# Neighbour counts turned by DMA transposes, and broadcast rows made by TensorE transposes, in a two-layer graph network kernel

## What is computed

```
x1  = layernorm(x + gcn(x, edges))           # normalised by degree, W is 768 x 768
h1  = relu(layernorm(gat(x1, W1, 4 heads x 256))) + x1 @ Wr1 + br1
h2  = layernorm(gat(h1, W2, 1 head x 768)) + h1 @ Wr2 + br2
out = layernorm(x1 + h2)

gat: xl = x @ W;  a_src, a_dst = sums of xl with two vectors, for each head
     e  = leaky_relu(a_src[src] + a_dst[dst], 0.2)
     softmax of e over the edges into each dst, then the weighted sum of xl[src], plus a bias
```

## Time and profile before

| | |
|---|---|
| three runs | 844.8, 844.95, 847.12 us; median 844.95 |
| the profiled execution | 844.18 us, its span 842.3 us, so 1.9 us lie around the span |
| mean granted TensorE clock | 0.994 |
| PE busy | 808.9 us, 96% of the span |
| DVE busy | 672.1 us, 80% |
| ACT, POOL busy | 268.8 and 60.1 us |
| DMA | 73.55 MB, 87 GB/s over the span |

### The profile page before, as it was taken

How to read it: one execution, slowest core, us unless ns; L and a number is a source line. 1 busy time by engine, 2 the same in 40 slices (tenths; PEclk the granted TensorE clock), 3 DMA queues, 4 the chain that set the end, 5 groups by cost and what they waited for, 6 DMA issues and landing times.

```text
span 842.3 us, 13750 instructions
## 1 busy us (share of the span) xinstructions
PE 808.9 (96%) x5022; PEld 533.0 (63%) x5022; DVE 672.1 (80%) x1181; ACT 268.8 (32%) x510; POOL 60.1 (7%) x81
## 2 busy tenths in 40 slices
PE   5899998999999999999999998999999999999995
PEld 4577774665554444447888887886666666555553
DVE  7999995777676659999988879969872287996686
ACT  2454456010011201015555455643301107760000
POOL 3000002011103000000000000011110000001111
PEclk9999999999999999999999999999999999999998
DMA  8000004041131353235212104113223342112232
GB/s 306 7 2 2 2 3 170 25 162 57 45 156 70 100 178 124 82 120 201 61 59 86 53 1 138 57 63 126 88 63 94 124 137 76 65 57 75 75 113 71
DMA packets 24588, 73.55 MB, mean 87 GB/s; under 512 B 2756, under 2 KB 3756, under 8 KB 24398
## 3 DMA queue, kind: packets, MB, share of 16 engines
q1 hardware_dynamic: 23262, 67.61, 23.3%
q0 software_dynamic: 1264, 5.11, 1.8%
HBM read 52.40 MB, written 20.31 MB: 86 GB/s over the span
## 4 chain that ended last, share of the span: by engine, by line
PE 89%; DVE 5%; issue 3%; DVEq 2%; ACT 1%; DMA 0%; POOL 0%; SPq 0%; POOLq 0%
PE psum L957 19%; PE psum L984 19%; PE psum L750 18%; PE psum L1065 12%; PE psum L872 8%; PE psum L762 6%; PE psum L814 3%; PE psum L972 1%; PE psum L998 1%; DVEq L1359 1%; PE psum L909 1%; PE psum L937 1%; ACT arena L1072 1%; PE psum L807 1%; PE psum L723 1%
## 5 line engine op out<-in xcount | busy, mean ns | idle before, releaser
L984 PE MATMUL psum<-arena 128*128 128x257 f32 x800 | 175.4, 381 | 2.6 <-DVE arena L1601 1.6
L1072 ACT ACTIVATE arena<-psum 128x160 f16<-128x160 f32 (+6 forms) x188 | 93.4, 528 | 258.9 <-PE psum L750 74.8
L984 PEld LDWEIGHTS psum<-arena 128*128 128x128 f32 x800 | 151.2, 190 | 26.2 <-ACT arena L1072 2.7
L750 PE MATMUL psum<-arena 128*128 128x512 f16 x720 | 159.3, 379 | 2.3 <-DVE arena L1429 1.9
L957 PE MATMUL psum<-arena 128*128 128x512 f16 x960 | 158.5, 326 | 0.2 <-ACT arena L1072 0.2
L957 PEld LDWEIGHTS psum<-arena 128*128 128x128 f16 x960 | 93.5, 97 | 62.3 <-ACT arena L1072 0.5
L750 PEld LDWEIGHTS psum<-arena 128*128 128x128 f16 x720 | 69.3, 98 | 86.4 <-issue 7.0
L1065 PE MATMUL psum<-arena 128*128 128x512 f16 (+2 forms) x600 | 98.4, 326 | 0.0
L1065 PEld LDWEIGHTS psum<-arena 128*128 128x128 f16 x600 | 58.3, 97 | 39.8
L1457 DVE CUSTOM_DVE_ANT_0 arena<-arena 128x1280 bf16<-128x1280 bf16 x50 | 71.0, 1488 | 14.1 <-DMA arena<-as_scratch 8.2
L1175 ACT ACTIVATE arena<-arena 128x640 f32<-128x640 f32 x80 | 64.5, 836 | 49.4 <-DVE arena L1586 49.2
(11 more groups left out here) (173 smaller groups left out, 714.9 us busy)
## 6 DMA issues: line engine op xcount, KB each, us to landing
arena<-in_L_gnn_W_dram SPq DMA_DIRECT2D x22, 384.0 KB, 3.2
r_scratch<-arena SPq DMA_DIRECT2D x10, 512.0 KB, 2.6
arena<-uv_scratch SPq DMA_DIRECT2D x16, 320.0 KB, 4.4
arena<-r_scratch SPq DMA_DIRECT2D x10, 512.0 KB, 3.7
x_scratch<-arena SPq DMA_DIRECT2D x10, 384.0 KB, 4.5
arena<-x_scratch SPq DMA_DIRECT2D x10, 384.0 KB, 3.5
r_scratch<-arena SPq DMA_DIRECT2D x10, 384.0 KB, 2.6
arena<-r_scratch SPq DMA_DIRECT2D x10, 384.0 KB, 3.7
```

The costliest lines, as they stand in the source:

```text
L750: ins = pe.matmul(o[:, a:b], part[:, k, ds(t * P, P)], w[:, k, a:b], start=(not begun and k == 0 and n == 0 and m == 0), stop=(k == kn - 1 ...
L984: last = pe.matmul(p_att[:, ATT_BANKS[ch][j], 0:HID + 1], pf[n % PSLOTS][:, j * P:(j + 1) * P], xl[ch % H][:, k, 0:HID + 1], start=(k == 0 ...
L1072: act.activation(out_, in_, ACT.Copy, scale=scale).then_inc(signal, 1)
```

## The change

- `c_hi` is stored whole to HBM (`c_d`) after the third load of W1. When the first aggregation is over, ten DMA transposes (`dma_start_transpose`, 128 rows x 1280 columns each) bring it back turned, as `c_turned`, f16 at 70 KB, in the place of `c_lo`.
- The ten `neg` steps leave `X1_ORDER`. `tr 2` now stands after tile 0, `tr 3` after tile 1.
- `mask` reads `c_turned` in SBUF instead of PSUM, and writes `neg` over it. Its wait is for all ten transposes. Four masks stand after the eviction of tile 2, three after tile 3, three after tile 4 (`MASKS_AT`).
- `xl_evict(0)` stands directly behind tile 0's sums, and waits for the store of `c_hi`.
- On SP the store of the masks moves behind the first two loads of Wr1.
- `rows_of` uses `pe.transpose` instead of `pe.matmul`, with the same operands.

```
-        X1_ORDER += [s for k in range(KD) for s in [("part", 0, k)] + ([("neg", k - 3)] if k >= 3 else [])] + [("xl", 0)]
-        X1_ORDER += [s for k in range(KD) for s in [("part", 1, k)] + [[("neg", 3)], [("tr", 2)], ...][k]] + [("xl", 1)]
+        X1_ORDER = [("tr", 0), ("tr", 1)] + [("part", 0, k) for k in range(KD)] + [("tr", 2), ("xl", 0)]
+        X1_ORDER += [("part", 1, k) for k in range(KD)] + [("tr", 3), ("xl", 1)]
...
             sp.wait_ge(S["h_done"], T)
-            weights(1)
+            weights(1, range(3))
+            sp.wait_ge(S["blk_free"], NB)
+            sp.dma_start(c_d, c_hi.rearrange("p t n -> p (t n)")).then_inc(S["c_out"], 16)
+            weights(1, range(3, KD))
...
+            sp.wait_ge(S["c_out"], 16)
+            sp.wait_ge(S["gcn_done"], T)
+            for k in range(T):
+                sp.dma_start_transpose(c_turned[:, :, k * P:(k + 1) * P], c_d[:, k * NP:(k + 1) * NP]).then_inc(S["c_turn"], 16)
+            sp.wait_ge(S["x1_out"], 16 * T)
+            sp.wait_ge(S["x1_tr"], T)
+            weights(2, range(2))
             sp.wait_ge(S["neg_ok"], T)
             sp.dma_start(neg_d, neg.rearrange("p t n -> p (t n)")).then_inc(S["neg_out"], 16)
-            sp.wait_ge(S["x1_out"], 16 * T)
-            sp.wait_ge(S["x1_tr"], T)
-            weights(2)
+            weights(2, range(2, KD))
...
-                elif what == "neg":
-                    slot_read(t, used[t % 2])
-                    for k in range(T):
-                        last = pe.transpose(p_neg[t % 2][:, k * P:(k + 1) * P], c_hi[:, k, t * P:(t + 1) * P], ident_h)
-                    last.then_inc(S["neg_tr"], 1)
-                    used[t % 2] = (what, t)
...
-                    last = pe.matmul(o[:, i * P:(i + 1) * P], column[:, t:t + 1].to_broadcast([P, P]), ident, start=True, stop=True)
+                    last = pe.transpose(o[:, i * P:(i + 1) * P], column[:, t:t + 1].to_broadcast([P, P]), ident)
...
-                dve.wait_ge(S["neg_tr"], t + 1)
-                dve.tensor_scalar(neg[:, t, :], p_neg[t % 2], 0.0, NEG_BIG, ALU.is_equal, ALU.mult).then_inc(S["neg_ok"], 1)
+                dve.wait_ge(S["c_turn"], 16 * T)
+                dve.tensor_scalar(neg[:, t, :], c_turned[:, t, :], 0.0, NEG_BIG, ALU.is_equal, ALU.mult).then_inc(S["neg_ok"], 1)
...
                 elif what == "xl":
-                    if t == 1:
-                        dve.wait_ge(S["par_b1"], 16)
-                        xl_evict(0)
                     dve.wait_ge(S["xl_done"], t + 1)
                     project(t, H, HID, p_x[t % 2], a_junk)
-                    if t:
-                        xl_evict(t)
+                    if t == 0:
+                        dve.wait_ge(S["par_b1"], 16)
+                        dve.wait_ge(S["c_out"], 16)
+                    xl_evict(t)
+                    for m in MASKS_AT.get(t, ()):
+                        mask(m)
```

More of the change, by code:

```diff
@@ L89 @@
 AHEAD_R = 2
+MASKS_AT = {2: range(0, 4), 3: range(4, 7), 4: range(7, T)}
 WR1_AT = {5: (0,), 6: (1, 2), 7: (3,), 8: (4, 5)}
@@ L261, in gnn_program @@
         x1_sb = x_sb
+        c_turned = at(70 * KB, [T, NP], f16)
         neg = at(70 * KB, [T, NP], bf16)
@@ L336, in gnn_program @@
         p_deg, p_flag = bank(7, 2 * T), psum[0:1, 512 * 7 + 32:512 * 7 + 33]
-        p_neg = [psum[:, 512 * i:512 * i + NP // 2].bitcast(f16) for i in (6, 0)]
         p_out = [psum[:, 1024 * i:1024 * i + D] for i in range(2)]
@@ L351, in gnn_program @@
         r2_d = nc.dram_tensor("r2_scratch", [T, P, D], f32).ap()
+        c_d = nc.dram_tensor("c_scratch", [P, T * NP], f16).ap()
         neg_d = nc.dram_tensor("neg_scratch", [P, T * NP], bf16).ap()
@@ L365, in gnn_program @@
             w_in0 w_in1 w_in2 w_in3 w_in4 w_in5 w_hi w_lo clo_ok deg_done dinv_ok over_ok flag_done flag_ok
-            neg_tr neg_ok gcn_done gcn_read gcn_var gcn_rstd x1_ok x1_out
+            c_out c_turn neg_ok gcn_done gcn_read gcn_var gcn_rstd x1_ok x1_out
             x1_tr x1t_hi_ok x1t_lo_ok as_ok as_tr as_rows as_dram asr0 asr1 max_ok
@@ L405, in step_count @@
             return steps_done, enter_loop, leave_loop
-        X1_ORDER = [("tr", 0), ("tr", 1)]
-        X1_ORDER += [s for k in range(KD) for s in [("part", 0, k)] + ([("neg", k - 3)] if k >= 3 else [])] + [("xl", 0)]
-        X1_ORDER += [s for k in range(KD) for s in [("part", 1, k)] + [[("neg", 3)], [("tr", 2)], [("neg", 4), ("tr", 3)], [("neg", 5), ("neg", 6)], [("neg", 7)], [("neg", 8), ("neg", 9)]][k]] + [("xl", 1)]
+        X1_ORDER = [("tr", 0), ("tr", 1)] + [("part", 0, k) for k in range(KD)] + [("tr", 2), ("xl", 0)]
+        X1_ORDER += [("part", 1, k) for k in range(KD)] + [("tr", 3), ("xl", 1)]
         X1_ORDER += [s for i in range(2, T) for s in [("tr", t) for t in (2 * i, 2 * i + 1) if t < T] + [("xl", i)]]
@@ L643, in _ @@
             param("par_b1", b1, 2)
-            pool.wait_ge(S["neg_tr"], T)
+            pool.wait_ge(S["gcn_done"], T)
+            pool.wait_ge(S["c_out"], 16)
             pool.wait_ge(S["w_lo"], W_FIRST[2])
@@ L890, in slot_read @@
             def slot_read(t, last):
-                if last and last[0] == "neg":
-                    pe.wait_ge(S["neg_ok"], last[1] + 1)
-                elif last:
+                if last:
                     pe.wait_ge(S["x1t_lo_ok"], last[1] + 3)
@@ L1485, in _ @@
                     x1t_low(t)
-                elif what == "neg":
-                    mask(t)
                 elif what == "xl":
-                    if t == 1:
-                        dve.wait_ge(S["par_b1"], 16)
-                        xl_evict(0)
                     dve.wait_ge(S["xl_done"], t + 1)
                     project(t, H, HID, p_x[t % 2], a_junk)
-                    if t:
-                        xl_evict(t)
+                    if t == 0:
[4 more added lines that the diff above has]
+                        mask(m)
                     weights(2, WR1_AT.get(t, ()))
```

## The result

The changed kernel takes **836.93 us**, the median of 4 runs (836.0 to 838.46), against 846.0 us of the kernel before on the same chip (844.8 to 847.12). The ratio is 0.9895, with a 95% interval of 0.9871 to 0.9919: faster by 9.1 us, 1.1%. Forecast were 834.0 us and a gain of 10.7 us in the trace; the profiled spans differ by 8.1 us.

The account below looks back on a forecast made before the run. TensorE, holding 89% of the chain, was taken as the bound. 842.3 - 7.3 - 3.4 = 831.6 us of span, 833.5 for the profiled execution, 834.3 on the median's scale; said 834.0, range 832.0 to 852.0.

Parts of the forecast that it names:

- Part 1: TensorE's path through x1 @ W1: without the count transposes tile 4 starts at 245.6 instead of 252.92, a gain of 7.3 us.
- Part 2: VectorE in x1 @ W1: masks of 0.82 us each fit beside TensorE's tiles and cost nothing; b1 has 9 us to spare.
- Part 3: Storing the counts to HBM, 3200 KB in 9.0 us, costs nothing, with 20 us of cover before SP's next load.
- Part 4: The ten DMA transposes before the masks: taken to land within 28 us of issue, so no stall of TensorE.
- the rivals: For the transposes: landing 28.4 to 39 us after issue, late yet a gain (13%); from 39 us, slower than before (22%).
- mostly bytes: Argument on the DMA transposes: a packet's time is mostly bytes, so a 256 B run costs far less than 0.135 us.
- the forecast deadline: The last DMA transpose may land at 240.0, 28.4 us after issue; each later microsecond costs TensorE one.
- the 22% for a loss: Rival at the first mask: transposes land 39 us or more after issue, making the kernel slower, 859.6 to 914 us; chance 22%.
- Part 5: Broadcast rows in layer two: ten transposes take 1.09 us instead of 2.23, saving 3.4 us over three calls.
- all that hangs on the end of tile 9 moves with it: After x1 @ W1: sums, their row over HBM, Wr1 products and attention all start earlier by the full 7.3 us.
- the second attention near 723.3: Sign in layer two that the forecast holds: the second attention starts 10.7 us earlier, near 723.3.
- a gain given back before 733: Sign of being wrong: the gain in x1 @ W1 is lost again before 733 on the trace's clock.

Follow-up runs that it names:

- b_same: The kernel before with nothing changed, run again for a second trace: 846.48 us, ratio 1.001 to before.
- rows_only: The kernel before with only the broadcast rows made by transposes instead of products: 842.18 us, ratio 0.9961 to before.
- late_turn: The changed kernel with five of the ten DMA transposes sent twice, the masks waiting for the second set: 840.57 us, ratio 0.9937 to before.
- store_first: tr3_early with the 40 KB store of the finished row issued ahead of two weight loads on SP: 836.28 us, ratio 0.9879 to before.
- tr3_early: The changed kernel with tile 3's transposes put in the middle of tile 1's matmuls: 833.63 us, ratio 0.9857 to before; repeated, 835.14 us, 0.9867.

## Why the prediction was nearly right, point by point

**Part 1, TensorE's path: right.** Tile 4 was forecast for 245.6 and came at 246.13. The 0.5 us are 0.13 us of the wait of `tr 5` (1.33, not 1.2), 0.2 of its own length (0.85, not 0.65), 0.13 in tile 0 and the rest in hundredths.

**Part 2, VectorE: right in its result, with a term too large.** The masks cost 0.42 us each and not 0.82; the nearer row was the one within SBUF, 648 elements in 324 ns, and even the 0.64 us by that row are half as much again as was measured. Since they were hidden, nothing came of it but 1.6 us of slack. b1 needed 5.8 us instead of 3.7 and had 9 to spare.

**Part 3, the store of the counts: nothing, as said.** It took 14.7 us where 9.0 were taken from the store of the masks, and so landed at 151.6, 14 us ahead of SP's next load. The cover did it, not the estimate.

**Part 4, the transposes: right, and the rivals fell.** Landing 22.6 us after the issue, within the 28.4. The argument that a small run costs less than the mean packet held (0.028 against 0.135 us); that its cost is "mostly bytes" did not: at 145 GB/s with full engines it costs 2.6 times what its bytes cost at the 383 GB/s of the earlier trace rows. The margin was 5.8 us against the forecast deadline, so the 22% for a loss were not foolish. The Trainium skill's *DMA: Bandwidth & Descriptors* ("Latency and other measured facts") with its 261 GB/s, which the page gives for a non-contiguous middle dimension, gave 12.6 us by the estimate in part 4; measured were 22.6, and the 12.8 us are what a plain load of the same bytes took here. The Trainium skill's *VectorE: DVE Perf Modes* ("The three transpose paths") with 1309 ns a block gave 131 us by the other estimate there; measured were 0.226 us a block, a hundred blocks in 22.6 us. For this stream of ten pieces neither figure holds, and the measured one decides.

**Part 5, the broadcast rows: right to the hundredth.** 1.09 us a call, 3.43 us in three calls, in every pair of traces with and without them. The Trainium skill's *TensorE: Matmul & The Clock Gate* (terms table) would have made it 0.56 us by its factor of four, an estimate; the trace shows 2.05 times (2.23 against 1.09 us), not four times.

**The step that failed: "all that hangs on the end of tile 9 moves with it".** It moved, but not by as much. In the profiles of before and after, from tile 4 to the attention:

| event | before | after | earlier by |
|---|---|---|---|
| tile 4 | 252.92 | 246.13 | 6.8 |
| first maximum (`as_scratch` is back) | 312.90 | 307.36 | 5.5 |
| store of the finished row issued | 371.92 | 366.11 | 5.8 |
| its load issued | 375.46 | 370.81 | 4.7 |
| attention | 383.76 | 379.08 | 4.7 |

1.3 us went with the first trip of the row over HBM and 1.2 us with the store of the second; 0.3 us came back between, where the kernel before had let TensorE finish its matmuls ahead of the row. I had read the chain of before, seen only TensorE in it, and took what ran beside it for covered. It had no cover, as VectorE's timeline of the kernel before shows:

```profile
380.40 2.48 DVE L1586 SCALAR_TENSOR_TENSOR arena<-arena 128x640 f32<-128x640 f32 x3 [0.30 <-DMA arena<-uv_scratch]
```

VectorE did wait for the row, 0.30 us, and with 2.48 us for these and 0.75 for the next step its factors were ready at 383.6, a tenth or two before TensorE was free. The sum should have held a term of 0 to 2 us for that. Some of the 2.1 us is that the first trace of before caught short transfers; the measured times, from several runs each, show a gain of 9.1 us, 1.6 us short of the forecast.

The means of the traces have the same size. From tile 4 to the attention the three with counts turned by TensorE (before, `b_same`, `rows_only`) take 131.85 us and the nine with DMA transposes 133.4. Of these 1.55 us, 1.0 lies between the issue of the two weight loads and the landing of the second store (4.66 against 5.68, two groups that don't touch), and 0.6 in the first trip up to the first maximum (8.3 to 9.6 against 8.8 to 10.3 us, two groups that overlap, so this part may be spread). The maxima between them take the same time in all twelve. The cause of the 1.0 us is not settled.

**The numbers.** 836.93 lies 2.9 us above the 834.0 said, inside the range of 832.0 to 852.0. Of the 2.9 us, 1.6 are the gain that fell short; 1.0 is the kernel before, which measured 846.0 this time and not 844.95; and 0.3 is that the sum gave 834.3 and I said 834.0. The forecast "the second attention near 723.3" was missed by 2.6 us, and the sign that I named for being wrong, a gain given back before 733, showed itself for 2.1 of 6.8 us.

## What to carry to other kernels

Before a gain on the bounding engine is added to the sum, follow what depends on its result to the next place where the engine needs an answer, and compare the two arrivals there, in more than one trace if the path goes over HBM: a chain that reads "TensorE alone" can have another one a tenth of a microsecond behind it. Work that TensorE does only to move data, such as turning a matrix, is worth its own time when a DMA can do it and the reader comes 20 us later; lay out the deadline of that reader first, since the slack decides and not the rate. And where a wait of some 2 us stands ahead of a TensorE stage, look at the granted clock behind it before you price the wait at its length: in two traces here it cost 1.7 us beside itself, in others nothing.

## What the runs showed of the chip

- A DMA transpose of 16-bit data from HBM to SBUF, in 128 x 1280 pieces: at most 0.028 us of engine time for a run of 256 B, 145 GB/s for ten in a row with the engines full, 4.3 to 6.7 us from issue to landing. On SP each instruction took at least 1.33 us for 128 x 1280 and 1.27 us for 128 x 640; a plain load of the first size took 0.49 us by the median.
- A transpose whose operand is one broadcast f32 column takes TensorE 0.109 us for 128 x 128, as one of a full block does, and half of the f32 product.
- A store of 40 KB to HBM took 2.9 to 5.0 us, and the first load of it back to all partitions 4.4 to 7.7 us in the chains shown. Between traces of the same kernel the first load from `as_scratch` differed by up to 0.8 us (4.9 and 5.7 in before and `b_same`), and the whole trip, store and load, by up to 1.3 us.
- TensorE's granted clock fell to 0.50, the 1.2 GHz level, after waits of 1.95 us in `late_turn` and 2.6 us in `store_first` ahead of the first attention, not after 1.8 us in `tr3_early` and 1.2 us in after. Where it fell, the way from the first attention to the second was 1.65 to 1.7 us longer. Two traces on one side set no limit.
